# A vision-transformer layer in eight groups of images: where the last attention's class values, counts and shared product stand on TensorE

## The reference

```python
tokens = einsum('bpi,hi->bph', patches, W) + b          # 64 patches of 2352 values
h = concat([class_token, tokens], 1) * pos_embed
q, k = relu(n @ Wq.T + bq), relu(n @ Wk.T + bk)         # n = layernorm(h), split into heads
attn = softmax(einsum('bhnd,bhmd->bhnm', q, k) / (k.sum(-1) + eps))
h = h + (attn @ v) @ Wo.T + bo
out_shared = swiglu(flat @ shared_in_w.T) @ shared_out_w.T + shared_out_b   # flat = layernorm(h)
routed = cnt @ expert_out_bias + sum_e comb[:, e] * (swiglu(flat @ expert_in_w.T) @ expert_out_weight[e].T)
h = h + out_shared + routed                             # cnt, comb: top 2 of 4 experts of a chosen group
```

## Time and profile before

| | |
|---|---|
| median of 3 executions | 461.81 us (461.53 to 463.44) |
| the profiled execution | 458.87 us, of which the span 457.0 us |
| PE busy | 434.9 us, 95% of the span |
| DVE busy | 308.6 us, 68% |
| ACT busy | 189.9 us, 42% |
| POOL busy | 181.8 us, 40% |
| TensorE clock granted | 0.996 of full speed over the span |

### The profile page before, as it was taken

How to read it: one execution, slowest core, us unless ns; L and a number is a source line. 1 busy time by engine, 2 the same in 40 slices (tenths; PEclk the granted TensorE clock), 3 DMA queues, 4 the chain that set the end, 5 groups by cost and what they waited for, 6 DMA issues and landing times.

```text
span 457.0 us, 6933 instructions
## 1 busy us (share of the span) xinstructions
PE 434.9 (95%) x2313; PEld 305.9 (67%) x2313; DVE 308.6 (68%) x896; ACT 189.9 (42%) x358; POOL 181.8 (40%) x220
## 2 busy tenths in 40 slices
PE   6969999899999999999999999999999999999993
PEld 2435455656786677767886588567866778778672
DVE  0152476477766966596848685777678867986586
ACT  1015523753266415742384217532664138531530
POOL 7112721222165316532473127410662264505555
PEclk9999999999999999999999999999999999999998
DMA  8999655234103620074005510360000000000001
GB/s 328 394 391 359 208 162 178 72 116 146 62 1 105 215 71 0 2 250 140 0 1 156 185 49 1 124 195 2 2 18 6 1 1 1 1 25 1 0 14 37
DMA packets 16451, 45.96 MB, mean 101 GB/s; under 512 B 1904, under 2 KB 7584, under 8 KB 16416
## 3 DMA queue, kind: packets, MB, share of 16 engines
q1 hardware_dynamic: 14704, 43.50, 28.1%
q10 hardware_dynamic: 1712, 2.02, 1.3%
HBM read 43.39 MB, written 2.13 MB: 100 GB/s over the span
## 4 chain that ended last, share of the span: by engine, by line
PE 74%; DVE 12%; issue 5%; DMA 4%; POOL 2%; ACTq 1%; ACT 1%; DVEq 0%; POOLq 0%
PE acc L482 22%; PE B L468 5%; PE O L576 5%; DMA bq_row<-in_bq_row 4%; PE scores L702 2%; PE scores L546 2%; PE scores L704 2%; PE scores L703 2%; PE C L702 2%; PE C L704 2%; PE C L703 2%; PE B L525 2%; PE C L634 2%; PE B L511 1%; PE scores L634 1%
## 5 line engine op out<-in xcount | busy, mean ns | idle before, releaser
L482 PE MATMUL acc<-x_main,w_patch 128*128 128x512 f32 x288 | 140.8, 612 | 5.9 <-DMA w_patch<-in_w_patch 4.2
L482 PEld LDWEIGHTS acc<-x_main,w_patch 128*128 128x128 f32 x288 | 51.0, 194 | 48.3 <-issue 38.5
L1884 POOL TENSOR_TENSOR prod<-prod 128x512 f32<-128x512 f32 x31 | 40.0, 1289 | 27.7 <-DVE q_nat L1324 10.6
L992 ACT ACTIVATE probs_t<-B 128x512 f32<-128x512 f32 x32 | 19.1, 596 | 50.1 <-PE B L468 50.1
L576 PEld LDWEIGHTS O<-v_bd,probs_t 128*128 128x128 f32 x256 | 31.9, 192 | 10.4 <-issue 7.7
L1877 POOL TENSOR_TENSOR hidden_lo<-silu,hidden_hi 128x512 fp32r<-128x512 f32 x16 | 20.3, 1271 | 40.7 <-ACT hidden_hi L992 40.7
L576 PE MATMUL O<-v_bd,probs_t 128*128 128x64 f32 x256 | 31.6, 271 | 0.0
L1819 POOL TENSOR_TENSOR rstd<-var,neg_half 128x4 f32<-128x4 f32 x8 | 8.1, 1018 | 50.8 <-DVE var L1281 50.8
L992 ACT ACTIVATE probs<-shift 128x512 f32<-128x512 f32 x32 | 20.1, 627 | 18.9 <-DVE shift L1337 16.8
L992 ACT ACT_TABLE_LOAD x19 | 24.4, 1283 | 7.4 <-issue 7.0
L702 PE MATMUL scores<-w_eout_hi,hidden_hi 128*128 128x512 f32 x64 | 27.3, 426 | 0.0
(11 more groups left out here) (334 smaller groups left out, 1005.1 us busy)
## 6 DMA issues: line engine op xcount, KB each, us to landing
x_main<-in_x_main SPq DMA_DIRECT2D x40, 768.0 KB, 4.3
x_main<-in_x_main SPq DMA_DIRECT2D x8, 512.0 KB, 4.3
x_main<-in_x_main SPq DMA_DIRECT2D x8, 256.0 KB, 3.2
x_tail<-in_x_tail SPq DMA_DIRECT2D x8, 224.0 KB, 4.7
out_tokens<-y_out SPq DMA_DIRECT2D x14, 128.0 KB, 3.0
prod<-in_w_eout SPq DMA_DIRECT2D x2, 512.0 KB, 14.0
w_patch<-in_w_patch ACTq DMA_DIRECT2D x5, 192.0 KB, 10.9
silu<-in_w_in SPq DMA_DIRECT2D x2, 256.0 KB, 12.9
```

The lines of the kernel that those rows point to most:

```text
L482: last = mm(acc[:, :], w_patch[:, j, :], x_main[:, j, :], start=(j == 0), stop=False)
L992: return nc.scalar.activation(dst, src, func, **kw)
L1884: q.tensor_tensor(p[r, 0, :], p[r, 0, :], p[r, 1, :], ALU.add).then_inc(tree1_done.sem, 1)
```

## The change

On PE, the last group's list only: the 11 early pairs of class values go, and all 32 pairs stand behind `out_proj`, in four calls of 10, 10, 6 and 6 pairs between the experts 2 to 6. `counts(L-1)` and both parts of `shared_t(L-1)` go to the place between `score(L, 1)` and `prob_transpose(L, 0)`, with the banks B0 and B1 for their results. `expert` 1 goes ahead of `attn_transpose`. `shared_natural` goes behind `expert` 3, `ffn_in(L, 0)` behind `expert` 5, `gates(L)` behind `expert` 6, and `ffn_in(L, 1)` follows it directly.

On ACT the copy of the early values goes; `counts_out` and `shared_out` of group 6 move ahead of `probs_out(L, 0)`; `hidden_high` moves from before the exponential table's load to behind `probs_out(L, 0)`, `route_exp` and `class_exps` to behind `exps(L, 3)`. On POOL `hidden_low` moves behind `bias_residual`. On DVE `class_softmax(1)` stands ahead of `output(L-2)`, `weigh` 0 ahead of `shared_add`, and `class_own` has two products instead of three and waits for the last class value alone. No work is added.

```diff
@@ -53,3 +53,2 @@
 AHEAD = 6
-EARLY = 11
 PIECES = [(0, 1), (1, 3)] + [(j, j + 3) for j in range(3, NMAIN, 3)]
@@ -232,3 +231,2 @@
         tc_soft = [sb("tc_soft", [128, 2, NPATCH]), x_main[:, 8, 0:2 * NPATCH].rearrange("p (a m) -> p a m", m=NPATCH)]
-        tc_val = x_main[:, 8, 256:256 + EARLY * HEADS]
         tc_cc = sb("tc_cc", [128, 4])
@@ -310,4 +308,4 @@
         tsc_full, tmax_step, texp_done, tsum_step = ev("tsc_full"), ev("tmax_step", 4), ev("texp_done", 2), ev("tsum_step", 6)
-        tpr_full, tpr_done, tval_full, tval_done = ev("tpr_full"), ev("tpr_done"), ev("tval_full"), ev("tval_done")
-        town_step, tout_full = ev("town_step", 5), ev("tout_full")
+        tpr_full, tpr_done, tval_full = ev("tpr_full"), ev("tpr_done"), ev("tval_full")
+        town_step, tout_full = ev("town_step", 4), ev("tout_full")
         ecls_full, prodcls_done, treecls_step = ev("ecls_full", 2), ev("prodcls_done", 2), ev("treecls_step", 3)
@@ -394,2 +392,4 @@
         def shared_bank(g):
+            if g == GROUPS - 2:
+                return B0
             return B0[:, 384:512] if is_class(g) else B0 if g == GROUPS - 1 else C0
@@ -397,2 +397,4 @@
         def shared_t_bank(g):
+            if g == GROUPS - 2:
+                return B1
             return B0[:, 256:384] if is_class(g) else B0 if g == GROUPS - 1 else C0
@@ -555,4 +557,8 @@
                     need(pe, v_done, g)
+                    if g == GROUPS - 1:
+                        need(pe, cnt_done, g - 1)
                 elif p == 1:
                     need(pe, q_done, g)
+                    if g == GROUPS - 1:
+                        need(pe, sht_done, g - 1)
                 else:
@@ -568,4 +574,2 @@
                         pe.wait_ge(tmax_step.sem, 4)
-                    elif g == GROUPS - 1:
-                        pe.wait_ge(tval_done.sem, 1)
                 elif p == 2:
@@ -605,3 +609,3 @@
                 elif not is_class(g):
-                    pe.wait_ge(town_step.sem, 5)
+                    pe.wait_ge(town_step.sem, 4)
                 plain = z_sides(g)[2]
@@ -620,2 +624,3 @@
                     need(pe, h2_done, g)
+                    need(pe, ysh_done, g - 1)
                 elif is_int(g, GROUPS - 1) and k == 1:
@@ -643,2 +648,4 @@
                     need(pe, hid_done, g, 3)
+                elif is_int(g, GROUPS - 2):
+                    need(pe, v_done, g + 1)
                 elif not is_class(g):
@@ -661,2 +668,4 @@
                         need(pe, h2_done, GROUPS)
+                    elif g == GROUPS - 2:
+                        need(pe, q_done, g + 1)
                     else:
@@ -672,2 +681,4 @@
                 need(pe, sht_done, g)
+                if g == GROUPS - 2:
+                    need(pe, h2_done, g + 1)
                 for t in range(tiles):
@@ -692,3 +703,3 @@
                         need(pe, nat_done, g + 2)
-                elif u == 3:
+                elif u == 3 and g < GROUPS - 2:
                     need(pe, ysh_done, g)
@@ -729,15 +740,11 @@
 
-                need(pe, tpr_done, 1 if end > IMAGES // 4 else 0)
-                if first >= EARLY:
-                    need(pe, o1_done, GROUPS - 1)
-                else:
-                    pe.wait_ge(tmax_step.sem, 8)
+                need(pe, tpr_done, 1)
+                need(pe, o1_done, GROUPS - 1)
                 for pair in range(first, end):
-                    for b2, bank, col in ((0, acc, pair * HEADS), (1, O, pair * HEADS + (128 if pair < EARLY else 0))):
+                    col = pair * HEADS
+                    for b2, bank in ((0, acc), (1, O)):
                         r = slice(64 * b2, 64 * b2 + 64)
-                        last = mm(bank[:, col:col + HEADS], v_bd[r, pair, b2, :, :].rearrange("p h c -> p (h c)"),
+                        mm(bank[:, col:col + HEADS], v_bd[r, pair, b2, :, :].rearrange("p h c -> p (h c)"),
                                   tc_prob_t[r, pair * HEADS:(pair + 1) * HEADS], start=True, stop=True)
-                if end == EARLY:
-                    last.then_inc(tval_full.sem, 1)
-                elif end == IMAGES // 2:
+                if end == IMAGES // 2:
                     pe.wait_ge(cdve.sem, 20)
@@ -924,6 +931,6 @@
             ffn_in(L - 1, 3, TOK)
-            class_values(0, 5)
             score(L, 0)
             score(L, 1)
-            class_values(5, EARLY)
+            counts(L - 1, TILES, 128)
+            shared_t(L - 1, TOK)
             prob_transpose(L, 0)
@@ -935,26 +942,24 @@
             prob_transpose(L, 2)
-            shared_t(L - 1, TOK, (0,))
             prob_transpose(L, 3)
-            counts(L - 1, TILES, 128)
             prob_v(L, 2)
             prob_v(L, 3)
-            shared_t(L - 1, TOK, (1,))
             expert(L - 1, 0, 128)
+            expert(L - 1, 1, 128)
             attn_transpose(L)
-            shared_natural(L - 1, TILES, 128)
             out_proj(L)
             class_probs(1)
-            expert(L - 1, 1, 128)
-            class_values(EARLY, 17)
             expert(L - 1, 2, 128)
-            class_values(17, 23)
-            z_transpose(L)
+            class_values(0, 10)
             expert(L - 1, 3, 128)
-            class_values(23, IMAGES // 2)
-            ffn_in(L, 0, TOK)
+            shared_natural(L - 1, TILES, 128)
+            class_values(10, 20)
+            z_transpose(L)
             expert(L - 1, 4, 128)
-            gates(L, TILES, 128)
+            class_values(20, 26)
             expert(L - 1, 5, 128)
-            ffn_in(L, 1, TOK)
+            ffn_in(L, 0, TOK)
+            class_values(26, IMAGES // 2)
             expert(L - 1, 6, 128)
+            gates(L, TILES, 128)
+            ffn_in(L, 1, TOK)
             ffn_in(L, 2, TOK)
@@ -1142,6 +1147,2 @@
 
-            def class_values_out():
-                act.wait_ge(tval_full.sem, 1)
-                go(tc_val[:, :], O[:, 128:128 + EARLY * HEADS]).then_inc(tval_done.sem, 1)
-
             def attention_filled(g, par, last):
@@ -1214,11 +1215,10 @@
             silus(L - 1, 3, TOK)
-            hidden_high(L - 1, 0, TOK)
-            hidden_high(L - 1, 1, TOK)
             load_table(L, 1, ACT.Exp)
+            counts_out(L - 1, TOK)
             exps(L, 0)
-            class_values_out()
             exps(L, 1)
+            shared_out(L - 1, TOK)
             probs_out(L, 0)
-            route_exp(L - 1, TILES, 128)
-            class_exps(1)
+            hidden_high(L - 1, 0, TOK)
+            hidden_high(L - 1, 1, TOK)
             probs_out(L, 1)
@@ -1226,6 +1226,6 @@
             exps(L, 3)
+            route_exp(L - 1, TILES, 128)
+            class_exps(1)
             probs_out(L, 2)
             probs_out(L, 3)
-            counts_out(L - 1, TOK)
-            shared_out(L - 1, TOK)
             attn_out(L)
@@ -1644,13 +1644,10 @@
 
-                dve.wait_ge(tval_full.sem, 2)
-                dve.wait_ge(tval_done.sem, 1)
-                first = EARLY * HEADS
-                for b2, src, a, b in ((0, acc[:, 0:256], 0, IMAGES // 2), (1, tc_val, 0, EARLY),
-                                      (1, O[:, first:256], EARLY, IMAGES // 2)):
-                    v.tensor_tensor(tc_own[:, b2, a:b], src.rearrange("p (a h) -> p a h", h=HEADS),
-                                    const[:, C_HEAD:C_HEAD + HEADS].unsqueeze(1).to_broadcast([128, b - a, HEADS]),
+                dve.wait_ge(tval_full.sem, 1)
+                for b2, src in ((0, acc[:, 0:256]), (1, O[:, 0:256])):
+                    v.tensor_tensor(tc_own[:, b2], src.rearrange("p (a h) -> p a h", h=HEADS),
+                                    const[:, C_HEAD:C_HEAD + HEADS].unsqueeze(1).to_broadcast([128, IMAGES // 2, HEADS]),
                                     ALU.mult).then_inc(town_step.sem, 1)
-                dve.wait_ge(town_step.sem, 3)
+                dve.wait_ge(town_step.sem, 2)
                 v.tensor_reduce(tc_own_sum[:, :, :], tc_own[:, :, :, :], AX.X, ALU.add).then_inc(town_step.sem, 1)
-                dve.wait_ge(town_step.sem, 4)
+                dve.wait_ge(town_step.sem, 3)
                 v.tensor_tensor(tc_attn_t[:, :].rearrange("p (a b) -> p b a", b=2), tc_own_sum[:, :, :],
@@ -1760,4 +1757,4 @@
             attn_sum(L, 1)
-            output(L - 2, TILES, 128)
             class_softmax(1)
+            output(L - 2, TILES, 128)
             residual(L, 1)
@@ -1766,4 +1763,4 @@
             norm2_scale(L, h2[1], TILES, 128)
-            shared_add(L - 1, h2[0], TILES, 128)
             weigh(L - 1, 0, 128)
+            shared_add(L - 1, h2[0], TILES, 128)
             weigh(L - 1, 1, 128)
@@ -1956,6 +1953,6 @@
             expert_sum(L - 2, 2, 128)
-            hidden_low(L - 1, 0, TOK)
-            hidden_low(L - 1, 1, TOK)
             expert_sum(L - 2, 3, 128)
             bias_residual(L, 1)
+            hidden_low(L - 1, 0, TOK)
+            hidden_low(L - 1, 1, TOK)
             class_value(L, 0)
```

26 lines of the change are left out of this document (13 added, 13 removed).

## The result

| | before | changed |
|---|---|---|
| median | 461.67 us | 467.45 us |
| lowest to highest, 4 executions each | 460.33 to 463.44 us | 465.17 to 469.72 us |
| the profiled execution | 458.87 us (span 457.0) | 469.70 us (span 467.9) |
| TensorE clock granted in it | 0.996 | 0.979 |

The changed kernel is slower, by a ratio of 1.0136 [1.0094, 1.0178], which is 6.3 us. The forecast was 4.16. The median says less than it seems to: the four executions are two at 465.2 and two at 469.7, and none lies near the 467.45 between them, so that it came within 1.5 us of the forecast 466.0 is in part luck. In every run here the medians take in all executions; the ratio and its interval leave out single ones more than 1.5% above the fastest of their kernel.

A forecast was written before the change was run, and what follows sets the result against it. It took DVE to bound the last attention and PE the late stretch; after the change, DVE's queue behind `class_own` delays `class_out` by 4.16 us, so 461.81 + 4.16 = 466.0 us, range 463.4 to 467.5.

The forecast's parts named there:

- Parts 1 and 2: Last attention: first transposition 0.44 us later, at 390.38; DVE still ends the attention, so `class_probs(1)` moves to 404.36.
- Part 3: PE from `class_probs(1)` to the last class value: 5.93 us more work ahead, start at 420.44 instead of 414.07.
- Part 4: `class_own` on DVE: removed operation takes off 0.66 us, longer second product adds 0.10; 1.74 instead of 2.30.
- the other price (2.23): Removed operation's 88 columns scaled from 168 columns, worth 0.17 us: `class_own` 2.23 and the sum 0.49 more.
- Part 5: DVE's work queued behind `class_own` starts at 422.65 and PE waits for it; `class_out` starts 4.16 us later.
- Part 6: From `class_out` to the end nothing changes, so the 4.16 us carries through: 466.0 for the median.
- A (PE alone): Late stretch: DVE's queue is through in time and PE sets the end, `class_out` 2.1 later, 463.9 us; chance 0.16.
- B: PE, not DVE, ends the attention, so filling its hole takes 2.24 us off; 0.6 faster, 461.2 us; chance 0.06.
- C: In the attention POOL's `hidden_low` holds DVE's `row_sum`, up to 1.04 us more: 467.0 us; chance 0.10.

## Why the prediction was half right

**Direction, and the order of the list: right.** Slower (chance 0.78), by 4.16 us of order: at a like mean clock 3.8 to 4.1 were measured. What the forecast didn't have is the clock.

**Parts 1 and 2, the attention: right.** The first transposition was forecast at 390.38 and came at 390.44; `class_probs(1)` 404.36 and 404.37. DVE still ends the attention: PE's wait before `attn_nat`'s transposition is 0.26 where it was 0.50, and its releaser is the same. Nothing was given back.

**Part 3, the last class value: wrong.** The work in the sum was sized well: at the lower clock a pass takes 0.43 us to the next row for 0.23, so 10.2 us there lose 10.2 x (1 - 0.23 / 0.43) = 4.7, and 425.21 less that is 420.5, for a forecast of 420.44. But it came at 425.21. (That every instruction in the stretch slows as those passes do is my assumption.) The step that failed is that every term was a duration from the earlier trace rows, all at a granted clock of 1.00, added up as if the clock there were given. I read PE as full in the earlier trace rows and took "full" for "safe". A term was missing: 4.77 us, a clock at half for 10.2 us. It was in no rival either. The Trainium skill ("TensorE: Matmul & The Clock Gate", What's actually happening) says that the clock gate goes by how busy the PE has been recently. Read with the profile's busy share, the trace doesn't agree (10.00 of 10 us busy at 0.78 in the changed kernel, 8.03 of 10 at 1.00 without the products); the runs with and without the small products say that those are what parts the two.

**Part 4, class_own: right.** 1.73 against 1.74, in every profile with the two products, so the whole 0.66 was the length of the removed operation, and the other price (2.23) was not. How long that operation takes goes by POOL. In the kernel with filled holes the same 88 columns took 0.38 us, and 32 columns beside an idle POOL, in the kernel with four early pairs, 0.18:

```profile
413.57 1.27 POOL L1886 TENSOR_TENSOR prod<-prod 128x512 f32<-128x512 f32 x1
414.57 0.38 DVE L1652 TENSOR_TENSOR x_main<-x_main,const 128x88 f32<-128x88 f32 x1
```

```profile
420.47 0.18 DVE L1664 TENSOR_TENSOR x_main<-x_main,const 128x32 f32<-128x32 f32 x1
```

With filled holes it ends at 414.95, 0.11 behind POOL's operation; in the kernel before at 415.63, 0.11 behind POOL's L1886; in the kernel with one long call 0.11 behind, in the one with 25 late pairs 0.08. So POOL held it, and the 0.66 was what it cost in that place, not a fixed price.

**Part 5, the queue: right but for the last wait.** The distances on DVE are, from the last class value, gates' wait 0.47 (0.6 forecast), 0.36 before `ffn_in(L, 1)` (0.4), logits to `weigh` 4 430.81 - 429.78 = 1.03 (1.05), to `hidden_mul` 1 2.65 (2.65), then 0.60 and 0.76 (0.59 each). The wait before `class_out`, nearly 1 by the forecast, is gone: the second low stretch slows PE by 3.4 x (1 - 0.23 / 0.43) = 1.6, that wait took up about half of it, and 0.82 is left. The other order of the tail shows the queue for itself: 2.3 to 2.5 us less at a like mean clock, for 2.0 expected, and 0.79 less in the runs without products, for about 1.

**Part 6, to the end: right**, -0.08.

**The rivals.** A (PE alone) needed no idle PE between 404 and `class_out`; the 0.47 and 0.36 stand there. B needed an attention that ends earlier against the scores; it is 0.58 longer. C needed a held `row_sum`. The line of the changed kernel, against the earlier trace rows:

```profile
L1349 DVE TENSOR_TENSOR row_sum<-patch_sum,exp_cls x16: 174/174/1214, 62.0 to 399.1; 128x16 f32<-128x16 f32 x16
```

It still has one long row, 1.21 us from 354.45, beside an operation of POOL from 354.36 to 355.63; the one in question, at 396.29, took 0.17.

**What was shown, and what stays open.** Shown: in the profiles the late fall comes with the small products (all out: 1.00 from 404 to 440; replaced by whole tiles: 1.00 until 424.2), is there in all six with 28 or 32 of 32 pairs behind the output projection, and doesn't need the new attention order. The mean clocks of the executions say the same, with one exception:

| late pairs | mean clock of single executions |
|---|---|
| 28 or 32 (five kernels, 24 executions) | 0.971 to 0.989, once 0.993 |
| 25 | 0.974 to 0.994 |
| 21 in one call | 0.975 to 0.986 |
| 21 spread (the kernel before) | 0.982 to 0.996, once 0.979 |
| 18, and 3 in holes | 0.982 to 0.997, once 0.975 |
| 32 pairs of whole tiles instead | 0.989 to 0.996 |
| none, tail in the other order | 0.992 to 0.996 |
| none | 0.979 to 0.995 |

The last row is the exception: four of nine executions without any products are at 0.982 or lower, and that stays unexplained. Density and amount both count: in the profiles 21 pairs in one call fall, 21 in three don't, 25 in three briefly do. Open: why executions of the changed kernel fall into two groups, 465.2 and 469.7; where the unprofiled executions lose their clock, of both kernels; what causes the short falls in the attention and in the patch projections; and what it is in the small products: their 64 rows, their 8 columns, their two passes, or that they aren't transpositions. These weren't tried apart. No kernel tried beat the one before by more than its measurement can tell, with the whole computation in it.

## What to carry to other kernels

Before adding durations from a trace, ask whether the rows were taken at a clock that the new order will keep: gathering many tiny products on a busy TensorE can cost more in clock than in time of their own (here 0.23 us each pair of products, and in the profile 5.6 us more for moving eleven of them and doing all 32 in four calls). Read the granted clock by stretches beside the busy share, in both profiles, and compare executions at equal mean clock. And where an in-order queue waits for one late value, price what stands behind it, not the value: here each step on DVE came out to within 0.2 us.

## What was unexpected of the hardware

The granted clock fell to half while PE was busy for 10.00 of 10 us, and stayed at 1.00 in a kernel where it was busy for 8.03. At the lower level a pass over 512 columns goes from 0.23 to 0.43 us to the next row, so the 10.2 us cost 4.77. With 64 transpositions of whole tiles in the same places (0.11 us apart) it stayed at 1.00 until 424.2, past the last of them. A DVE product with both operands in SBUF took 0.74 us for 88 columns in the kernel before and 0.38 with filled holes, and ended 0.11 us behind an operation of POOL both times. The early falls came in some profiles around 33 to 36 and 86 to 91 us and in others not at all, and cost 1.2 to 1.5 us each (the changed kernel 1.16, its repetition 2.85 for two): that alone makes the executions of one kernel differ by more than many a change is worth.
